# Two gated cross-attention and mixture-of-experts layers on one core: the second block list done two parts to a block, the last division ahead of the scatter slots, idle products around the first block, pads on two queues

## The reference

```python
x = x + jnp.tanh(g_xattn[0]) * _L0_xattn_ref(_layernorm(x, axis=-1), ctx_1024, ctx_1024, mask_Bx1x1xS2_ff0, ...)
x = x + jnp.tanh(g_ffn[0]) * _L0_ffn_ref(_layernorm(x, axis=-1), ...)
...
    # layer 0, for each expert e: 256 -> 688 -> 256
    h = jax.nn.silu(xf @ w_gate[e]) * (xf @ w_up[e])
    out = out + combine[:, e:e + 1] * (h @ w_down[e])
...
    # layer 1, for each expert: 256 -> 256 -> 256
    hidden = jnp.square(jax.nn.relu(hidden))
```

## Time and profile before

| | |
|---|---|
| timed runs, median of 3 | 770.54 us (769.27 to 770.83) |
| profiled execution, its own time | 775.69 us |
| its span, first to last instruction | 773.7 us |
| mean granted clock of PE | 0.966 |
| PE busy | 688.5 us, 89% of the span |
| DVE busy | 412.0 us, 53% |
| ACT busy | 279.1 us, 36% |
| POOL busy | 227.5 us, 29% |
| experts of layer 0 | about 161 to 487 us |
| experts of layer 1 | about 646 to 750 us |

### The profile page before, as it was taken

How to read it: one execution, slowest core, us unless ns; L and a number is a source line. 1 busy time by engine, 2 the same in 40 slices (tenths; PEclk the granted TensorE clock), 3 DMA queues, 4 the chain that set the end, 5 groups by cost and what they waited for, 6 DMA issues and landing times.

```text
span 773.7 us, 17602 instructions
## 1 busy us (share of the span) xinstructions
PE 688.5 (89%) x5858; PEld 523.2 (68%) x5858; DVE 412.0 (53%) x1377; ACT 279.1 (36%) x549; POOL 227.5 (29%) x409
## 2 busy tenths in 40 slices
PE   8799888799999799999999999879988778799970
PEld 6567666567777577777777777567766556578850
DVE  3888778854333323333332332568978776644426
ACT  4555556331211112111121121457755533245530
POOL 5124444341221101001011010214556435534440
PEclk9999999999999899999999999999989989899995
DMA  9244444451223301111011100511112123443428
GB/s 229 86 139 131 145 138 140 139 180 49 68 83 96 87 27 35 35 35 35 28 35 35 34 28 14 183 50 55 38 57 70 64 84 83 145 131 115 120 83 325
DMA packets 50856, 70.72 MB, mean 91 GB/s; under 512 B 7687, under 2 KB 38023, under 8 KB 50771
## 3 DMA queue, kind: packets, MB, share of 16 engines
q1 hardware_dynamic: 42380, 50.85, 21.7%
q0 software_dynamic: 6816, 18.69, 6.8%
q10 hardware_dynamic: 1575, 0.05, 0.2%
HBM read 46.55 MB, written 23.02 MB: 90 GB/s over the span
## 4 chain that ended last, share of the span: by engine, by line
PE 68%; DVE 12%; issue 6%; another core or an unknown queue 4%; DMA 3%; ACT 2%; SPq 2%; POOL 1%; DVEq 0%; POOLq 0%; ACTq 0%
PE ps L1646 26%; PE ps L1686 17%; PE ps L1439 4%; DVE m_rows L936 3%; PE ps L1665 3%; PE ps L1377 3%; PE ps L1431 2%; PE ps L1394 2%; PE ps L1477 2%; DVE x_sb L920 2%; PE ps L1453 2%; PE ps L1405 2%; DVE ctx_q L953 1%; DMA ys_dram<-share,dest_i 1%
## 5 line engine op out<-in xcount | busy, mean ns | idle before, releaser
L1646 PE MATMUL ps<-w_all,share 128*128 x780 | 230.2, 442 | 6.5 <-DVE share L1074 3.6
L1646 PEld LDWEIGHTS ps<-w_all,share 128*128 128x128 f32 x780 | 144.5, 191 | 68.5 <-issue 10.4
L593 POOL DMA_INDIRECT ys_dram<-share,dest_i x78 | 75.8, 971 | 322.2 <-DVE share L1241 271.2
L1686 PE MATMUL ps<-w_all,share 112*128 (+1 forms) x624 | 150.9, 385 | 2.9 <-ACT share L821 2.1
L1686 PEld LDWEIGHTS ps<-w_all,share 112*128 112x128 f32 (+1 forms) x624 | 114.8, 194 | 17.2 <-issue 4.0
L1298 DVE TENSOR_TENSOR share<-share,ps 128x344 f32<-128x344 f32 x78 | 40.1, 514 | 136.1 <-PE ps L1646 73.2
L804 ACT COPY share<-ps 128x512 f32<-128x512 f32 x39 | 22.8, 585 | 157.2 <-PE ps L1665 157.2
L936 DVE TENSOR_REDUCE m_rows<-ps 128x8 f32<-128x960 f32 x64 | 70.6, 1144 | 14.7 <-PE ps L1394 11.7
L799 ACT ACTIVATE share<-ps 128x344 f32<-128x344 f32 x78 | 35.7, 457 | 103.7 <-PE ps L1646 99.3
L564 POOL DMA_INDIRECT xs_dram<-xn,slot_now x64 | 63.8, 996 | 22.0 <-issue 14.3
L541 POOL TENSOR_SCALAR nm<-mv 128x1 f32<-128x1 f32 (+1 forms) x48 | 11.4, 237 | 166.3 <-DVE mv L976 128.7
(11 more groups left out here) (212 smaller groups left out, 1022.0 us busy)
## 6 DMA issues: line engine op xcount, KB each, us to landing
share<-xs_dram SPq DMA_DIRECT2D x78, 129.0 KB
w_all<-ys_dram SPq DMA_DIRECT2D x16, 512.0 KB, 6.7
w_all<-gate SPq DMA_DIRECT2D x8, 688.0 KB
w_all<-up SPq DMA_DIRECT2D x8, 688.0 KB
w_all<-down SPq DMA_DIRECT2D x8, 560.0 KB
w_all<-w SPq DMA_DIRECT2D x16, 256.0 KB
xs_dram<-q_flat SPq DMA_DIRECT2D x17, 129.0 KB
out<-x_sb SPq DMA_DIRECT2D x8, 256.0 KB, 5.5
```

Of the source, the lines that this page charges most:

```text
L593: g.indirect_dma_start(ys_dram, bass.IndirectOffsetOnAxis(ap=dest_i[:, u:u + 1], axis=0), y_sb[:, u, :], None).then_inc(D_y[u], 16)
L1646: i = t.matmul(ps[:, bank, 0:w], xgT[:, k, :], w_all[:, bass.ds(off + (k * UPW[l] + col - EW[l]), w)], start=(k == 0), stop=(k == KT - 1))
L1686: i = t.matmul(ps[:, 6, 0:D], hT[0:r, c + KD[1] * (j % 2) * l, :], w_all[0:r, bass.ds(off + (KT * UPW[l] + c * D - EW[l]), D)], start=(c = ...
```

## The change

In words, seven edits.

1. In layer 0 `list_rest` runs two parts to a block beside blocks 3 to 7, not one part beside each of blocks 3 to 11.
2. In the last attention unit of both layers DVE runs `divide` and `x_evac(0)` ahead of `logits_copy` and `route2`, not behind them.
3. In the same unit PE runs 2, 5 and 3 idle products around `route` and `block_t(0)`, not 4 between them.
4. Of the eight pads of a layer SP writes four, one behind each of four gathers, not two.
5. ACT writes the other four, at the end of its blocks 4 to 7 in layer 0 and 5 to 8 in layer 1.
6. In layer 1 PE runs the ranks of batch 6 in block 2, behind `down(0)`, not in block 1 ahead of `route`.
7. DVE's `route2` of that batch moves from `beside1(1)` to `beside1(2)`, behind `logits_copy`.

```diff
+        def write_pad(eng, e):
+            row = eng.value_load(pad_i[0:1, e:e + 1], min_val=0, max_val=NE * REGION - P)
+            eng.dma_start(xs_dram[bass.ds(row, P), :], zrow).then_inc(D_pad, 16)
...
-                for e in range(NE):
-                    if e % 2 == 0:
-                        load_block(N1 - 5 + e // 2)
-                    row = sp.value_load(pad_i[0:1, e:e + 1], min_val=0, max_val=NE * REGION - P)
-                    sp.dma_start(xs_dram[bass.ds(row, P), :], zrow).then_inc(D_pad, 16)
+                for e in range(NE // 2):
+                    load_block(N1 - 5 + e)
+                    write_pad(sp, e)
                 load_block(N1 - 1)
...
+                def last_pad(n):
+                    a.wait_ge(d_pad, l + 1)
+                    a.wait_ge(g_z, 2 * l + 2)
+                    write_pad(a, NE // 2 + n)
...
+                    if 4 <= j < 4 + NE // 2:
+                        last_pad(j - 4)
...
+                    if 5 <= j < 5 + NE // 2:
+                        last_pad(j - 5)
...
+                    if u == NU - 1:
+                        divide(G)
+                        x_evac(0)
                     if u >= 3:
                         logits_copy(G - 3, 1)
                     if not even and b >= 2:
...
-                    divide(G)
+                    if u < NU - 1:
+                        divide(G)
...
-                    if u == NU - 1:
-                        x_evac(0)
...
-                    if 3 <= j <= 11:
-                        list_rest(j - 3)
+                    if 3 <= j <= 7:
+                        for part in range(2 * (j - 3), min(2 * (j - 3) + 2, 9)):
+                            list_rest(part)
...
-                    if j == 1:
-                        route2(B1 - 1)
                     if j == 2:
                         logits_copy(G1 - 1, LAST_LOGITS[l][1])
+                        route2(B1 - 1)
...
                     if u == NU - 1:
+                        idle_products(2, 2)
                         route(G - 2, LAST_LOGITS[l][0])
-                        idle_products(4, 2)
+                        idle_products(5, 2)
                         block_t(0)
+                        idle_products(3, 0)
...
                     if j == 1:
-                        last_ranks(B1 - 1)
                         t.wait_ge(d_lg, G1 - 1)
                         route(G1 - 1, LAST_LOGITS[l][1])
+                    if j == 2:
+                        last_ranks(B1 - 1)
```

## The result

The changed kernel takes 766.61 us (median of 7 runs, 764.06 to 769.12), the kernel before beside it 770.83 us (median of 7). The ratio is 0.9937, 95% interval [0.9911, 0.9963]: 4.9 us faster, between 2.9 and 6.9. The forecast was 762.3 us with a range up to 766.5. The ratio on the 770.54 us from which it started gives 765.7, inside the range by 0.8; the median itself, 766.61, lies just outside. The sign was right, and of the forecast gain of 8.2 us some 3.4 are missing.

What follows compares the result with a forecast made beforehand. TensorE was taken as the limit, with a late gather in layer 0. From 775.69 us profiled, -7.1 + 0.4 - 3.0 + 0.3 + 1.2 = -8.2 gave 767.5, less 5.15 to the timed median: 762.3 us, range 758.3 to 766.5.

Steps and rivals of the forecast that it cites:

- the second list: Layer 0: the list ends earlier, so block 13's gather is no longer late; 7.1 us gained, bounds 5.0 and 7.13.
- So `up` comes 0.2 us later, not sooner: Block 0's start: one more idle product ahead of the transposes delays `up`; both layers +0.4 us, between 0 and 0.8.
- so I take the 3.4 us as caught up, at no price: Layer 1: batch 6's slots come 3.4 us later, but GpSimd's 14 indirect operations make up the pauses; cost zero.
- second rival: Layer 1 loses as GpSimd's operations stand without pauses; 769.1 us, or 767.0 or 765.8; chance 0.19 for 765 to 769.
- one such stretch more, 3 us, with its half clock: Layer 1: one more stretch with SP and ACT standing while GpSimd works, 3 us, plus 2.1 us of half clock.
- The late normalisation: Layer 1: late slots of batch 5 push back the last tile's normalisation and transposes; cost 1.2 us, between 0 and 2.1.
- The pads: Layer 1: four pads fewer on SP gain 3.0 us (1.3 to 4.5); ACT's pads cost 0.3 (0 to 0.6).
- its 5.1 us: The second rival's term for one more standing stretch and its half clock in layer 1; half of it gives 765.8 us.

Runs made afterwards that it cites:

- e3: The changed kernel with edit 2 undone in layer 1 alone; ratio to the kernel before 0.9916.
- e6: The changed kernel with TensorE's register load of block 0's weight offset taken ahead of its wait for DVE's read of the ranks; ratio to the kernel before 0.9950.
- e5: The changed kernel with edits 6 and 7 undone; ratio to the kernel before 0.9889.
- e7: The kernel before with edits 6 and 7 alone; ratio to the kernel before 1.0026.
- e9: The changed kernel with GpSimd, in layer 1, waiting until its store of block 0 has landed before batch 6's scatters; ratio to the kernel before 0.9949.
- e11: The kernel before with edits 1, 4 and 5 (list and pads), run a second time; ratio to the kernel before 0.9898.
- e1: The kernel before with edit 1 alone, the second list two parts to a block; ratio to the kernel before 0.9914.
- e2: The kernel before with edits 1, 4 and 5 (list and pads), first run; ratio to the kernel before 0.9900.
- e4: The changed kernel with all eight pads of a layer back on SP (edits 4 and 5 undone); ratio to the kernel before 0.9998.
- e8: The changed kernel once more, unaltered, for a second profile and comparison; ratio to the kernel before 0.9967.

## Why the prediction was right and wrong

**Right: the second list.** -7.1 us forecast, 7.1 us in the profile, 6.6 timed. The gather of block 13 was put at 242, 80.3 us behind block 0's `up`; it went out after 80.2. DVE's doubled list work was hidden: from block 4 on every `up` of layer 0 follows the one before it after 8.10 us.

**Wrong: "So `up` comes 0.2 us later, not sooner".** It came 1.14 us later in layer 0 and 1.24 in layer 1, 2.4 us in place of the 0.4. The idle products were costed right, at next to nothing (0.11 us in e3). The step that failed is the list of gates of block 0: I named the division and the transposes, and left out `t.wait_ge(d_rk, B1 - 1)`, at which TensorE stands behind the last unit, and beside it the one for the copy of the logits, `t.wait_ge(d_lg, G1 - 2)`, which has moved with it. Before, `rk` was read at 158.42, 3.3 us ahead of `up`, and the wait cost nothing. With the slots behind the division it comes last, and block 0's register load is queued behind it: e6 takes the load from behind the wait and gets 0.6 and 0.8 us back.

**Wrong: "so I take the 3.4 us as caught up, at no price".** The delay was larger than 3.4 us, and it wasn't caught up. Counted from block 0's `up` in layer 1 (646.60 before, 632.52 now), the first scatter of batch 6 goes out after 12.65 us in place of 7.45, and the last scatter of batch 7 after 34.23 in place of 28.94; the second profiles have 12.51 and 7.46, 34.94 and 28.15. It brought batch 6's scatters up against the stores of blocks 0 to 2, which had been spread out. I counted GpSimd's operations and saw room, and left out what the others lose while it has no pause. By e5 against the changed kernel the two edits cost 3.7 to 6.0 us timed (0.9889 against 0.9937 and 0.9967), the largest miss; without edit 2 they cost 2.0, not clear of nothing (e7). So the price is that of both delays together. e9 shows what the run of stores does to the engines at block 6, and also that breaking this one run doesn't win the time back: how much of the price is the run and how much the lateness of the scatters is not shown. It is the mechanism of my second rival, "one such stretch more, 3 us, with its half clock": the measured 766.61 lies in that rival's 765 to 769, which had 0.19.

**The late normalisation, +1.2.** Block 3 is 2.0 us later (10.71 against 8.71 in e5 and e11), nearer the bound of 2.1 than the 1.2 that I took, but block 13 isn't: alone it costs nothing, and with edits 6 and 7 it adds some 3 us (e3).

**The pads, -3.0 and +0.3.** TensorE's wait at the gathers is gone, as forecast; the net is 1.1 us by one pair (e1, e2) and 2.4 to 4.7 by the other (the changed kernel, e4), and layer 1's stretch shows neither (96.05 with the list alone, 94.42 and 96.87 with the pads), so -2.7 is neither confirmed nor refuted. ACT's pads show no sign of waiting for SP's issues. Here the two overlap, ACT's row and SP's:

```profile
656.33 0.34 ACTq L372 DMA_DIRECT2D xs_dram<-q_flat  x1
```

```profile
656.55 0.36 SPq L372 DMA_DIRECT2D xs_dram<-q_flat  x1
```

ACT's issue takes 0.34 us and ends at 656.67, SP's begins 0.12 us before that and takes its usual 0.36. The Trainium skill ("Perfetto Trace Analysis", section "DMA Instruction — HWDGE (DVE, Sync)") has the issuers lock the generator in turn. It names the sequencers of DVE and Sync; here they are ACT's and SP's. No cost of such a lock shows in these rows.

**The sum.** List and pads came out at 0.9899 (mean of e2 and e11), the changed kernel at 0.9952 (mean of its two): edits 2, 3, 6 and 7 together cost 0.53%, 4.1 us, where the forecast had 1.6 (0.4 + 1.2). The stretches give more, 2.4 us at the two starts and 4.9 in layer 1 (100.5 against 95.6, means of two profiles each), 7.3 in all. With single profiles 2.5 us apart and ratios uncertain by some 0.3%, how much between 4 and 7 is right stays open. One figure of the second rival doesn't follow from its terms: half of its 5.1 us gives 766.6, not 765.8.

## What to carry to other kernels

When an instruction is moved back on one engine, list every semaphore it raises, and for each the first wait on every other engine, with what is queued behind that wait, register loads too; the gate that had slack may be the one that closes. Count not only how much work an engine with indirect stores has, but how long it goes without a pause: work that is "caught up" without pauses may cost the others more than a late start. And time each edit alone before the bundle: here one of seven brought as much as all of them.

## What the runs showed that I had not expected

While GpSimd issues indirect stores back to back, 1.27 us apart, waits of DVE and ACT are let go late: with four in a row they stand for about 2 us (DVE 1.94 and ACT 2.27 in e5), with seven DVE for 4.9 to 6.4 and ACT for 3.9 to 6.1 (changed kernel, e3, e7, e8), and with a pause of 1.72 us after the third DVE for 0.78 (e9). The Trainium skill ("SBUF — State Buffer", section "SBUF: two separate sides") says of the memory's ports that ACT and TensorE never wait on anyone and that only VectorE and GpSimd lock each other out; here ACT stood for 6.06 us, so that rule doesn't cover it. What it is in the chip that holds the waits back was not found out.

With a register load on TensorE behind the semaphore wait the first product starts 1.12 to 1.25 us after the releasing instruction's end (changed kernel), and 0.30 to 0.33 us after it with the load taken ahead of the wait (e6): some 0.8 to 0.9 us for one load and its register operations.
